# A two-layer attention kernel: an order of its own at the layer change, two tiles' keys in one step, first placings ahead of query reads, and own buffers in the tail

## The reference

```python
xn = _layernorm(x, norm_scale, norm_bias)
q, k, v = xn @ Wq + bq, xn @ Wk + bk, xn @ Wv + bv
k = jnp.where(mask, -jnp.inf, k); v = jnp.where(mask, 0.0, v)
q = jax.nn.softmax(q, axis=-1)          # over the head's features
k = jax.nn.softmax(k, axis=2)           # over the positions
attn = jnp.einsum('bhse,bhsd->bhed', k, v)
y = jnp.einsum('bhtd,bhed->bhte', q, attn)
emb_out = jax.nn.silu(emb) @ film_emb_W + film_emb_b
scale, shift = jnp.split(emb_out, 2, axis=-1)
h = _layernorm(y) * (1.0 + scale[:, None, :]) + shift[:, None, :]
x = x + jax.nn.silu(h) @ film_out_W + film_out_b
```

## Time and profile before

| what | value |
|---|---|
| median of 3 runs | 894.03 us (892.1 to 894.65) |
| profiled execution | 891.59 us, span 889.8 us |
| TensorE busy | 846.5 us, 95% |
| VectorE, ScalarE, GpSimd busy | 76%, 68%, 62% |
| DMA | 169.79 MB, 191 GB/s |
| granted TensorE clock over the span | 0.99 |

### The profile page before, as it was taken

One profiled execution on the slowest core, in us unless ns is written; L12 is line 12 of the kernel. 1 busy time (PEld: TensorE's weight loads), 2 busy tenths in 40 slices (PEclk: granted clock), 3 DMA queues, 4 the chain that ended last, 5 costly groups with the idle time before them and its releaser, 6 DMA issues.

```text
span 889.8 us, 19791 instructions
## 1 busy us (share of the span) xinstructions
PE 846.5 (95%) x6581; PEld 715.5 (80%) x6581; DVE 680.7 (76%) x1350; ACT 608.3 (68%) x1445; POOL 553.6 (62%) x743
## 2 busy tenths in 40 slices
PE   4988999999999999999979999999999999999996
PEld 4867788888878788888757888888888888888875
DVE  6977777777777787778768887887788778776754
ACT  6355776776675777777767867776776777767654
POOL 2557667666756557766856776667666766676541
PEclk9989999999999999999989999999999999999999
DMA  8676675766666655555655656556566655665431
GB/s 292 237 257 193 204 237 183 215 206 208 185 208 189 184 204 170 179 171 185 193 170 178 208 173 206 185 174 199 188 193 196 197 190 182 192 197 180 159 119 48
DMA packets 115482, 169.79 MB, mean 191 GB/s; under 512 B 11806, under 2 KB 84630, under 8 KB 115382
## 3 DMA queue, kind: packets, MB, share of 16 engines
q1 hardware_dynamic: 114880, 168.08, 59.4%
q10 hardware_dynamic: 502, 0.46, 0.2%
HBM read 95.61 MB, written 72.88 MB: 189 GB/s over the span
## 4 chain that ended last, share of the span: by engine, by line
PE 72%; DMA 11%; DVE 5%; ACT 4%; issue 3%; SPq 2%; POOL 2%; ACTq 0%; POOLq 0%; DVEq 0%
PE PS L857 62%; PE PS L946 6%; PE PS L929 3%; DMA qy_turned<-QS 3%; DMA QT<-qy_turned 2%; DMA k_turned<-KT 2%; DMA EK<-k_turned 2%; DMA x_turned<-XS 1%; SPq L392 1%; DMA STAGE<-in_wk 1%; ACT Z L688 1%; ACT XF L740 1%; ACT SK L653 1%; DMA STAGE<-in_wv 1%; SPq L404 1%
## 5 line engine op out<-in xcount | busy, mean ns | idle before, releaser
L565 POOL TENSOR_TENSOR HL<-H,HH 128x512 fp32r<-128x512 f32 x60 | 77.6, 1293 | 206.1 <-ACT HH L721 202.8
L688 ACT ACTIVATE Z<-QT,FC,FA 128x128 f32<-128x128 f32 x240 | 99.1, 484 | 100.0 <-DMA QT<-qy_turned 99.9
L857 PE MATMUL PS<-XH,WH_k 128*128 128x256 f32 x512 | 151.6, 296 | 4.2 <-DVE WL_k L309 4.2
L857 PE MATMUL PS<-XH,WL_k 128*128 128x256 f32 x512 | 146.3, 286 | 0.0
L857 PE MATMUL PS<-XL,WH_k 128*128 128x256 f32 x512 | 146.2, 286 | 0.0
L857 PE MATMUL PS<-WH_o,HH 128*128 128x512 f32 x248 | 105.7, 426 | 14.2 <-issue 11.6
L758 ACT ACTIVATE XN<-X,NBX,RSX 128x512 f32<-128x512 f32 x60 | 48.8, 815 | 91.8 <-POOL NBX L514 91.8
L857 PEld LDWEIGHTS PS<-XH,WH_k 128*128 128x128 f32 x512 | 99.6, 195 | 4.9 <-issue 4.5
L857 PE MATMUL PS<-WH_v,XH 128*128 128x512 f32 x256 | 100.9, 394 | 2.8 <-DVE WL_v L309 2.7
L857 PE MATMUL PS<-WH_q,XH 128*128 128x512 f32 x256 | 100.7, 394 | 0.0
L653 ACT ACTIVATE SK<-SK,KN 128x128 f32<-128x128 f32 x256 | 98.9, 388 | 2.6 <-DVE KN L1149 2.6
(11 more groups left out here) (149 smaller groups left out, 2097.1 us busy)
## 6 DMA issues: line engine op xcount, KB each, us to landing
qy_turned<-QS SPq DMA_DIRECT2D x60, 512.0 KB, 2.9
QT<-qy_turned SPq DMA_DIRECT2D x240, 128.0 KB, 2.9
k_turned<-KT SPq DMA_DIRECT2D x32, 512.0 KB, 4.1
EK<-k_turned SPq DMA_DIRECT2D x128, 128.0 KB, 2.8
x_turned<-XS SPq DMA_DIRECT2D x30, 512.0 KB, 2.8
XT<-x_turned SPq DMA_DIRECT2D x120, 128.0 KB, 3.4
out_x<-X SPq DMA_DIRECT2D x32, 256.0 KB, 3.3
X<-in_x SPq DMA_DIRECT2D x9, 512.0 KB, 5.2
```

Of the source, the lines that this page charges most:

```text
L565: eng.tensor_tensor(hl_of(o), h_of(o), hh_of(o).bitcast(F32), ALU.subtract).then_inc(pool_hl, 1)
L688: z = eng.activation(Z[:, c * P:c * P + P].rearrange("p (q n) -> p q n", q=Q), src, ACT.Identity, bias=FC[l][:, c, b:b + 1], scale=FA[l][: ...
L857: mm = eng.matmul(dst, left[a](c), right[b](c), start=(c == 0 and a + b == 0), stop=(c == C - 1 and a == 1))
```

## The change

At the layer change every engine gets its own order in steps 31 to 34, written out. In step 32 TensorE does keys(32) and keys(33); the second goes to PSUM bank B_TY. All four loads of WV stand ahead of the query read of step 31, all of WQ ahead of the placing of keys. In step 33 the write and read of an x pair stand behind the placing of keys. The first two placings of keys (steps 1, 3) are written, and the reads of x of step 3 issued, in another place among the reads of queries. The folded FiLM sums leave the bank of mix. In the tail z of tiles 61 and 63 and y of tiles 61 and 62 get buffers of their own, and VectorE makes HH.

```diff
-        LOW_ON_DVE = [range(C), range(C), [1, 2, 3], [0, 2], [0, 2], [0, 1, 2], [0, 2], [0, 2]]
+        LOW_ON_DVE = [range(C), range(C), [1, 2, 3], [0, 2], [0, 2, 3], range(C), [0, 2], [0, 2]]
...
+                a = 0 if o == t0 else Q // 2
+                return XT[:, a:a + Q // 2, :, :, :].rearrange("p a t c n -> p (a t c n)")
             return XN[:, 1, :] if o == t2 else YN[:, :]
 
+        def z_of(o):
+
...
                     load_second_bias(2, pool_bo)
+                if s == B + 1:
+                    write_keys(s // 2)
                 write_qy(s)
...
+                if s <= 3 and s % 2 == 1:
+                    write_keys(s // 2)
+                if 3 < s < B - 1 or s > B + 1:
+                    for g in pairs:
                         read_x(g)
                 if s == B - 1:
-                    load_second(eng, 5, [0])
+                    load_second(eng, 5, [1, 0, 2, 3])
                 read_qy(s)
                 if s == B - 1:
-                    load_second(eng, 5, [1, 2, 3])
-                    load_second_bias(0, dve_v)
+                    for g in pairs:
+                        read_x(g)
                 if s % 2 == 1:
+                    if s > 3 and s != B + 1:
+                        write_keys(s // 2)
+                    if s == B - 1:
+                        load_second_bias(0, dve_v)
+                        load_second(eng, 6)
                     place_keys(s // 2)
+                if s == B - 1:
+                    load_second_bias(1, dve_q)
...
                 if s == 3:
+                    read_x(FIRST + 1)
                     wait_split(2)
                     load_x(5)
+                if s == B + 1:
+                    for g in pairs:
+                        write_x(g)
+                        read_x(g)
...
             for s in SLOTS:
+                if s == B:
+                    root_y(s - 3)
+                    h_low(s - 4)
+                    split_low(eng, 6, low_on_pool(6))
+                    x_low(s + 2)
+                    normalise_keys(s)
+                    root_x(s + 5)
+                    normalise_keys(s + 1)
+                    queries(s)
+                    continue
...
                     root_y(s - 3)
+                if s == B - 1:
+                    split_low(eng, 4, low_on_pool(4))
...
                     h_low(s - 4)
-                if s == B - 1:
-                    split_low(eng, 4, low_on_pool(4))
-                if s == B:
-                    split_low(eng, 6, low_on_pool(6))
...
+                if s == B - 1:
+                    norm_x(s + 4)
+                    film(o)
+                    norm_y(s - 3)
+                    exp_q(j)
+                    split_high(4, [0, 1])
+                    h_high(o)
+                    split_high(4, [2, 3])
+                    x_turned(m)
+                    exp_k(i)
+                    heads(j)
+                    split_high(5)
+                    continue
+                if s == B:
+                    film(o)
+                    values(i - 1)
+                    h_high(o)
+                    norm_y(s - 3)
+                    split_high(6)
+                    exp_q(j)
+                    norm_x(s + 4)
+                    x_turned(m)
+                    exp_k(i)
+                    heads(j)
+                    values(i)
+                    exp_k(i + 1)
+                    continue
...
+                if s == B + 2:
+                    film(o)
+                    h_high(o)
+                    norm_x(s + 4)
+                    norm_y(s - 3)
+                    x_turned(m)
+                    exp_k(i)
+                    exp_q(j)
+                    heads(j)
+                    values(i)
+                    continue
...
                     norm_x(4)
+                    conditioning_sums(0)
                     exp_k(2)
...
+                if s >= 3 and s in FILM_SLOTS:
+                    conditioning_sums(FILM_SLOTS.index(s))
                 if s == 0 or s >= 3:
                     exp_k(i)
-                if s in FILM_SLOTS:
-                    conditioning_sums(FILM_SLOTS.index(s))
...
+                for n in keys_at(s):
+                    exp_k(n)
+                if 0 <= j:
                     heads(j)
                 if s > 0:
                     values(i)
                 if s == 3:
                     split_high(3)
-                for n in keys_at(s):
...
+                if i == B + 1:
+                    eng.wait_ge(act_cp, len(FILM_SLOTS))
+                    eng.wait_ge(dve_film, len(FILM_SLOTS))
+                else:
+                    eng.wait_ge(dve_ka, i)
...
-                    dst = bank(B_K, cc * PAIR, PAIR)
+                    dst = bank(bank_k(i), cc * PAIR, PAIR)
...
-                eng.wait_ge(dve_film, sum(s <= j + 2 for s in FILM_SLOTS))
...
+                if n > 0:
+                    eng.wait_ge(dve_film, n)
...
-                    eng.wait_ge(dve_yr, FILM_SLOTS[n] - 2)
                 for c in range(FILM_STEPS[n][2] // P):
-                    mm = eng.matmul(bank(B_Y, FOLDED + c * B, B), Z[:, c * P:c * P + P], FOLD[:, :], start=True, stop=True)
+                    mm = eng.matmul(bank(B_TY, c * B, B), Z[:, c * P:c * P + P], FOLD[:, :], start=True, stop=True)
...
+                if s != B + 1:
+                    keys(i)
+                if s == B:
+                    keys(B + 1)
...
+            attention(t0)
             values(t2)
-            attention(t0)
+            mix(t0)
+            turn_queries(t1)
             queries(t2)
+            attention(t1)
             turn_y(t9)
-            turn_queries(t1)
-            mix(t0)
-            output(LAST_Y - 1)
-            attention(t1)
-            turn_queries(t2)
             mix(t1)
             turn_y(t0)
+            output(LAST_Y - 1)
+            turn_queries(t2)
             attention(t2)
             mix(t2)
+            turn_y(t1)
             output(t9)
...
+            def h_parts(o):
+
                 eng.wait_ge(dve_h, o + 1)
+                wait_hh_free(eng, o)
+                then(eng.tensor_copy(hh_of(o), h_of(o)))
                 eng.tensor_tensor(hl_of(o), h_of(o), hh_of(o).bitcast(F32), ALU.subtract).then_inc(dve_hl, 1)
...
+            turn_keys(1)
             turn_queries(0)
-            turn_keys(1)
...
+            keys(2)
             stat_x(5)
             zero_attention()
-            keys(2)
...
+                if s == B:
+                    add_x(s - 5)
+                    mixed(s - 3)
+                    h_mul(o)
+                    turn_queries(s - 1)
+                    keys(i)
+                    turn_y(s - 3)
+                    split_low(eng, 6, LOW_ON_DVE[6])
+                    values(i)
+                    stat_x(s + 5)
+                    turn_x(s + 4)
+                    key_sums(i)
+                    keys(i + 1)
+                    turn_keys(i)
+                    queries(i)
+                    key_sums(i + 1)
+                    continue
...
-                    turn_y(s - 3)
+                turn_y(s - 3)
+                if s == B - 1:
+                    split_low(eng, 4, LOW_ON_DVE[4])
...
+                if s == 3:
                     turn_keys(i)
                 for n in keys_at(s):
+                    keys(n)
                     turn_keys(i)
-                    keys(n)
-                if s != B - 1:
-                    queries(i)
+                    key_sums(n)
+                queries(i)
                 if s in FILM_SLOTS:
...
-                if s < NT - 2 and s != B:
+                if 3 < s < NT - 2:
                     turn_keys(i)
-                for n in keys_at(s):
-                    key_sums(n)
+                if s == B - 1:
+                    split_low(eng, 5, LOW_ON_DVE[5])
                 if s == 3:
                     split_low(eng, 3, LOW_ON_DVE[3])
+            turn_keys(t2)
             add_x(t9 - 2)
             mixed(t9)
-            turn_keys(t2)
...
             h_mul(t9)
-            h_low(t9)
+            h_parts(t9)
             add_x(LAST_Y - 1)
-            mixed(t1)
+            h_mul(t0)
             mixed(t2)
-            h_mul(t0)
-            h_low(t0)
+            h_parts(t0)
             add_x(t9)
```

142 lines of the change are left out of this document (77 added, 65 removed).

## The result

| kernel | median, us | runs | range |
|---|---|---|---|
| before | 893.7 | 6 | 892.1 to 894.65 |
| after | 889.55 | 6 | 887.9 to 892.45 |

The ratio is 0.9956, with an interval of 0.9937 to 0.9976: 4.1 us faster, where I had forecast 10.6. The direction was right and the time lies in the range; the size is well under half of what I forecast. The profiled execution of after took 892.45 us, the slowest of its six, and that of before 891.59, less than any of the six in the table. So the two spans (890.7 and 889.8) can't be compared, but steps can. I measure them from the start of one mix to the start of another. A full-speed step is 12.8 us.

The account below looks back on a forecast made before the run. TensorE, busy 846.5 us, was taken as the bound, with 43 us of idle and low-clock work to win. Start 1.5, FiLM 1.2, layer change 4.6 and tail 3.3 make 10.6 us: from 894.03 to 883.4 us, range 875.5 to 890.5.

Parts of the forecast that it names:

- The layer change: Steps 31 to 34: 8.9 us won at mix(30), 4.3 us paid back in steps 33 and 34, so 4.6 us.
- 3.2 us of waiting at mix(32): Step 34: TensorE waits 3.2 us for heads(32) behind XT(18), for 0.4 before: minus 2.8 us.
- the speed that I had counted as kept: Layer change: with no idle ahead of output(28), its matmuls keep full speed, 1.7 us counted of 2.1 at most.
- a gap before attention(30): Layer change: listed, with a gap before values(32), as a sign that the forecast is wrong; no size given.
- the second rival: Layer change: longer wait at mix(32), with a 5.63 us write of x, and a falling clock: 888 us, chance 0.15.
- the fourth's "nothing at the layer change": No-change rival: layer change gives nothing at mix(33), start and tail 1 us each: 892 us, chance 0.07.
- all that the two waits of steps 33 and 34 push on: Behind the waits of steps 33 and 34 (minus 1.1 and 2.8 us): a further minus 0.4 us.
- The start: Steps 1 to 5: mix(1) 2.2 us sooner, most of it waited away before output(0); 1.5 us, bounds 0 and 5.
- FiLM: Steps 9 to 21: the fold's wait falls away in three steps, 1.2 us, bounds 0.5 and 2.
- the sentence that the middle has its order and so its width: Elsewhere the change leaves the order alone but for FiLM steps; another width mid-layer would show the forecast wrong.
- The tail: Keys(63) placed 3.7 us sooner, mix(62) at 862.2 us, last matmul 3.3 us sooner; bounds 1 and 5.5.

Follow-up runs that it names:

- two pairs: The layer change's order with against without: change_only against the kernel before (1.0016), and filmlate2 against its partner with the old order (881.81 and 881.4 us).
- a third: after2 against no_change, the layer change's order on top of changed start and tail: 888.65 against 892.32 us.
- the pair: filmlate2 against the same kernel with the old order in steps 31 to 34, on one chip: 881.81 and 881.4 us, both 0.9912.
- after2: The changed kernel once more, unaltered, for a second profile: 0.9938 of the kernel before, 888.65 us.
- filmlate2: The changed kernel with the FiLM half loads issued one step later, measured a second time: 881.81 us, ratio 0.9912.
- eqfirst: The changed kernel with exp_q(32) ahead of x_turned(36) and exp_k(34) in ScalarE's step 34: ratio 0.9941.
- best: x18eqh_film with ScalarE's h_high(31) ahead of x_turned(37) in step 35: 879.4 us, ratio 0.9879.
- change_only: The kernel before with the new order of steps 31 to 34 alone: ratio 1.0016.
- x18eqh_film: The changed kernel with later FiLM loads, x pair 18 written before the placing of keys, exp_q(32) and heads(32) ahead of x_turned(36): 881.3 us, ratio 0.9826.
- start_film: start_only with the FiLM half loads issued one step later: ratio 0.9906.
- later loads: Edit in several kernels: SP issues the eight FiLM half loads (512 KB) one step later, behind the query read. On the kernel before alone: 0.9971.
- no_change: The changed kernel with the old order of steps 31 to 34; start, FiLM steps and tail as changed: 892.32 us, ratio 0.9973.
- tail_only: The kernel before with the new tail alone: ratio 0.9973.
- start_only: The kernel before with only the changed start and the folded FiLM sums in bank B_TY: ratio 0.9992.
- before_film: The kernel before with only the FiLM half loads issued one step later: ratio 0.9971.

## Why the prediction was wrong

**The layer change, 4.6 us forecast; nothing measured in two pairs, 3.7 in a third whose traces put most of it elsewhere.** This is the term that failed. The mechanism was right up to its end: output(28) and mix(30) sooner, 3.2 us of waiting at mix(32) forecast and 3.25 measured, with ScalarE behind XT(18). From the query write to XT(18) I had worked out 14.65 us; it took 15.2 (470.30 to 485.5). Three sizes were off.
- What was won first. Mix(30) I put 6.1 us sooner (8.9 with the keys(33) already done). Against mix(28) it came 4.1 us sooner in the pair, 4.7 in after2, 2.0 in after. SP needed 4.28 us for WV's four issues and read the queries at 440.45, not 437. It waits there for the low parts of WK. I had let GpSimd's one chunk end them, at 1.74 us, and given VectorE's three no time; GpSimd's took 1.29, but VectorE's took 1.77 us each, one after the other, the last from 438.2. VectorE's low parts of WV followed at 443.5 to 446.1, where I had them done near 444. So output(28) came 1.2 us late against mix(28). Then EK stands on the queue behind WQ, whose load takes 8.04 us in the chain; in after its reads take 4.7 to 6.0 us to land, and attention(30) waits 1.1 to 2.2 us for it in ten of the eleven traces with the order. In after the clock was low here too (0.92 from mix(29) to mix(30), 17.4 us busy for after2's 15.9 at full clock), so the speed that I had counted as kept, 1.7 us, was kept in only part of the traces. I had named a gap before attention(30) as a sign of error, and had given it no price.
- What was paid back. The wait at mix(32) had its size, but started from a later write (470.3 for 465.9; 3.2 us later against mix(28)), so mix(32) came 0.8 to 2.8 us sooner against mix(28) instead of 4.6.
- The clock. In filmlate2 the step behind the wait has a granted clock of 0.88 and is 1.65 us longer, all of it busy. The same step is at 0.81 to 0.88 in five of the seven traces in which mix(32) waits 2.4 us or more. In after the fall comes one step later, 14.47 us busy for 12.8, and in eqfirst there is none; best has no wait at mix(32) and 0.90 in that step. So the fall goes with the wait in most traces, and the wait isn't shown to be its only cause. I had put this into the second rival, together with a write of x of 5.63 us (it took 3.82).

So the second rival's clock and the fourth's "nothing at the layer change" are what happened. The idle time from mix(28) to mix(36) shows it in one number: 7.7 to 9.4 us in three traces of the old order with the old start and the old loads, 9.1 to 11.3 in three of the new (after, after2, change_only). Over all twenty traces it is 6.9 to 12.1 us without the order and 8.4 to 11.8 with it. It was moved.

How much room the chain has that feeds mix(32) shows only in part. From the last matmul of queries(32) over write, read and exponentials to mix(32) it takes 27.2 us in before, where TensorE waits 0.4 us just ahead of it, and 28.4 in after with its 3.25 us of waiting; a steady step of layer 1, in which TensorE waits for nothing, has 29.4. But x18eqh_film takes 26.6 and best 24.9, neither with a wait at mix(32). So the chain could be shorter than it was in after. The stretches from mix(28) to mix(32) and on to mix(36), by the same columns as above, in before:
```profile
426.55:489.55 63.00, 53.93 (x401) 44.67 (x400) 47.53 (x92) 43.59 (x100) 42.08 (x52) 0.95 0.60 184
489.55:541.27 51.72, 51.35 (x401) 43.81 (x400) 43.45 (x83) 38.84 (x92) 37.35 (x49) 1.00 0.60 189
```
in x18eqh_film:
```profile
419.67:478.16 58.49, 52.92 (x401) 44.40 (x400) 47.71 (x89) 42.00 (x94) 38.60 (x47) 0.97 0.63 190
478.16:533.86 55.70, 51.42 (x401) 43.83 (x400) 46.41 (x86) 40.59 (x99) 39.69 (x52) 1.00 0.58 184
```
and in best:
```profile
418.20:476.56 58.36, 52.72 (x402) 44.40 (x401) 48.02 (x89) 42.21 (x96) 38.45 (x46) 0.97 0.61 188
476.56:532.78 56.22, 52.99 (x401) 44.94 (x400) 45.70 (x86) 40.25 (x98) 39.65 (x52) 0.97 0.56 184
```
In these two mix(32) comes 4.5 us sooner than in before, which is what I had forecast, and the next four steps take 4.0 to 4.5 us longer: by waits in x18eqh_film, by waits and the clock in best. The prediction had 0.4 us for all that the two waits of steps 33 and 34 push on, and let the lead at mix(32) count as a lead of the kernel. That is the step that failed, beside the sizes above. Which chain sets the steps behind mix(32) isn't shown.

**The start, 1.5 us, and FiLM, 1.2.** The reading of the start was right: output(0) waits away the greater part (on the mean 2.4 of 3.2 us), and what remains at mix(4) is about 3 us over all traces (108.6 on the mean of fourteen with the new start, 112.0 of five without; start_film, with the new start and 110.9, is left out, and would make it 108.8). That is twice the 1.5 that I took. The FiLM term is right too: the four steps of 9 to 21 with a fold take 14.25 to 14.26 us in after, for 14.26, 14.70, 15.00 and 15.08 in before, 2.0 us where I had 1.2; but with later loads the old folds take 14.25 to 14.6. What failed is the sentence that the middle has its order and so its width. From mix(8) to mix(28) the traces with the old loads take 265.7 us on the mean with the new start and 262.7 with the old. I read it so: a lead of TensorE over the queue of transfers lasts only while that queue isn't late. With the old loads it is gone by mix(28): 428.2 us on the mean of eight traces with the new start, 427.9 of four with the old, each group spread over 6 us. By the timed runs it is worth between nothing (no_change over tail_only) and 2.3 us (start_only, if every run had the loss in the tail that its trace has). With later loads it stays: from mix(8) to mix(28) both starts take the same (258.2 us on the mean of seven, 258.5 in before_film), mix(28) starts at 419.6 for 421.4, and start and tail bring 7.0 us, where I had forecast 6.0 with FiLM.

**The tail, 3.3 us.** Right. From mix(60) to the end the traces take 34.2 to 34.3 us with it and 37.9 to 38.0 without (39.6 in the two kernels of the start alone); 3.7 us. Mix(62) is 5.1 us closer to mix(60) (forecast 4.8). Timed alone it gave 2.4 us, 0.4 to 4.5.

**The sum.** The tail's 3.7 us and nothing from the layer change leave 0.4 us of the measured 4.1 for start and FiLM. So of the missing 6.5 us 4.6 are the layer change's and 2.3 those of start and FiLM; the tail gave 0.4 more. This split rests on the tail as the traces have it; by the ratios of after2's set of runs (5.5 us for the whole, 2.4 for start and tail) it would leave the layer change 3.1. The rule of the Trainium skill on the clock (TensorE: Matmul & The Clock Gate, Part 1) had been given 1.7 us at most in the second rival; the 1.65 us of the fourth step have that size. On the one on GpSimd and VectorE sharing interfaces (GPSIMD Engine Reference, Specifications) I let it bear on WV alone; the three low parts of WK at 1.77 us against 0.81 for the quickest of the earlier trace rows are where it counted. WV's four, during which GpSimd in after had no operation with two inputs of this size, took 0.65 to 0.89 us each, so the trace agrees.

**What stays open.** Why the later loads bring up to 8.4 us on one chip and the kernel before only 2.6 on another: the chip and the start were not separated. Why after2 is 3.7 us faster than no_change, when the pair with later loads has no difference. And what holds output(31) after the waits before it are taken away.

## What to carry to other kernels

A wait removed in front of the bounding engine is worth only what the waits behind it leave of it. Price the whole passage, up to the step that has its normal width again, and not the first tile that comes sooner: here mix(32) could be had 4.5 us sooner, and 0 to 1 us was left at mix(36). A lead won early is kept only if the queue of transfers keeps up; look at each large load for the write that stands right behind it. And take the mean of several traces: with the same program from mix(8) to mix(28) that stretch took 262.7 to 268.0 us in eight traces.

## What the runs showed of the hardware

The write of queries (512 KB) lands later the closer it is issued behind a load of 512 KB on the same queue. Taken as the time from its issue to the issue of the read that waits for it, it is 6.0 to 6.6 us when issued 0.5 us behind the load (queries 18 in eight traces), 4.9 to 6.1 at 1.0 to 1.2, 3.4 to 5.7 at 1.3 to 1.8, 3.0 to 4.1 at 1.9 to 2.4, and 2.6 to 3.5 with none for 19 us or more, but for one of 4.7. I had taken the page's median of 2.9 us for all.

VectorE's low part of a weight chunk (128x512, two inputs) took 1.74 to 1.78 us for WK in after, beside a low part, HL and XL on GpSimd (1.29, 1.75 and 1.57 us), and 0.65 to 0.89 us for WV, beside GpSimd's operations with one input.

The same kernel differs from chip to chip and from one set of runs to the next: the kernel before took 889.5, 890.4, 894.8, 897.1 and 897.5 us in five sets on four chips (894.8 and 897.1 on one of them), while the changed kernel with later loads took 881.8 beside the 889.5 and 884.1 beside the 897.1.
